# Splitting the scores of a five-block tile into products of 384 and 256 columns

## The chip, the core and the metric

The program runs on one core of a Trainium2 chip. The metric is the time of one execution on the device in microseconds; several executions are timed and their median is given. One further execution was recorded by the hardware profiler, and all rows below come from it.

## What is computed

Two layers over x of shape (2, 1024, 256): a linear attention layer, which the change leaves alone, and a transformer block with causal softmax attention (32 query heads, 8 key/value heads, 64 per head) and a mixture of experts. Each layer is added to x through a layer norm. The part that the change touches:

```python
q = (h @ wq).reshape(b, s, NH, D).transpose(0, 2, 1, 3)
k = (h @ wk).reshape(b, s, NKV, D).transpose(0, 2, 1, 3)
k = jnp.repeat(k, GROUPS, axis=1)            # 4 query heads share a key head
scores = jnp.einsum('bhqd,bhkd->bhqk', q, k) / jnp.sqrt(jnp.float32(D))
scores = jnp.where(causal, scores, jnp.finfo(scores.dtype).min)
attn = jax.nn.softmax(scores, axis=-1)
out = jnp.einsum('bhqk,bhkd->bhqd', attn, v)
```

## The kernel before

Each engine has one program of its own; semaphores order them. The softmax attention is a loop over 16 sequences (8 key/value groups times 2 batches), and each sequence has 8 tiles of 128 queries. Tile t belongs to sequence n = t // 8 and has ct = t % 8 in it; being causal, it attends to ct + 1 blocks of 128 keys. Four heads share each tile. The tile with five blocks is ct = 4.

Step t of the loop on TensorE interleaves three tiles by a fixed order in the source: score(t, 0), values(t - 2), score(t, 1), turn_part(t - 1, 0), score(t, 2), turn_part(t - 1, 1), project_out(t - 2), score(t, 3), turn_part(t - 1, 2), and a projection for a later half sequence. turn_part transposes normalised probabilities, block by block, four heads each (L1346); values multiplies them with v (L1358); project_out is L1367; the projection is L1295, or two transposes at L1285.

A score keeps float32 accuracy by splitting: query and key are each held as a rounded part and its remainder. The stationary operand holds the query's two parts stacked on 128 partitions, and two products accumulate into PSUM, one with khi (L1329) and one with klo (L1330), both of type fp32r. One product can write at most one bank of 512 columns. A tile with up to four blocks has one pair of products of up to 512 columns in a bank of its own per head; a tile with five or more has a pair of 512 columns and a pair with the rest, in two adjoining banks that heads 0 and 2, and 1 and 3, share. khi and klo have place for three halves of a sequence: the first half of even sequences lies at column 0, of odd ones at 512, and the second half of either at 1024 (place_in_half). Blocks 0 to 3 are the first half, block 4 begins the second.

VectorE (DVE) takes each head's scores with one masked maximum (L924), which also moves them to SBUF; ScalarE (ACT) takes the exponential (L673) and copies transposed blocks (L685); DVE normalises (L932). In step t DVE does maximum(t, 0), normalise(t - 1, 2) and (t - 1, 3), a part of the projected item (L907, L912 or L917), maximum(t, 1), maximum(t, 2), normalise(t, 0), the sum of the output (L961), maximum(t, 3), normalise(t, 1). The first transpose of a tile waits until all four heads of it are normalised (semaphore probs_ready). Other products that are named below: L1249 (linear attention) has a moving operand cut in short runs, by `vp[:, b, 4 * k:4 * (k + 1), 0:4:3]`; L1444 is the experts' first product, 128 columns in one run.

Of the kernel before, what the change touches and what calls it, by code (L numbers as in the profile page):

```python
# [14 lines left out]
P = 128  # L15
D = 256
KB = D // P
BATCH, SEQ = 2, 1024
NT = BATCH * SEQ // P
TB = SEQ // P  # L20
# [13 lines left out]
HALF = SEQ // 2  # L34
PAIRS = TB * (TB + 1) // 2
EPS = 1e-5
MASKED = -1e30
# [44 lines left out]
def place_in_half(n, half):  # L82

    return 2 * HALF if half else n % 2 * HALF


def build(nc, a, out):
    ctx = ExitStack()
    with ctx:
# [10 lines left out]
        def turned_bank(t, k):  # L100

            return wide[:, 2 * t + k, :] if t < 2 else bank[2 * (t - 2) + k][:]

        def score_bank(t, h):

            if t % TB < TB // 2:
                return wide[:, h, :]
            return wide[:, 2 * (h % 2):2 * (h % 2) + 2, :].rearrange("p a b -> p (a b)")
# [15 lines left out]
        def S(name):  # L124

            if name not in sems:
                sems[name] = ctx.enter_context(nc.semaphore(name))
            return sems[name]
# [22 lines left out]
        def part(at, n, pattern, **dims):  # L151
            return arena[:, at:at + n].rearrange(pattern, **dims)
# [23 lines left out]
        at = 10 * KB * D  # L176
        n = KB * BATCH * HB * P
# [14 lines left out]
        at = 14336  # L192
# [34 lines left out]
        probs = [part(i * G * SEQ, G * SEQ, "p (h m) -> p h m", h=G) for i in range(2)]  # L227
# [10 lines left out]
        causal = part(4 * G * SEQ + 8 * P, SEQ, "p (o c) -> p (o c)", o=1)  # L238
# [56 lines left out]
        with ExitStack() as early:  # L295
            def sb_early(name, shape, dt):
                return early.enter_context(nc.sbuf_tensor(name, shape, dt))

            khi = sb_early("khi", [P, 3 * HALF], F32R)
            klo = sb_early("klo", [P, 3 * HALF], F32R)  # L300
# [231 lines left out]
        def _(act):  # L532
# [177 lines left out]
            for t in range(NT // 4):  # L710
                act.wait_ge(S("hT_psum"), 2 * t + 1)
                nc.scalar.copy(hT[:, 0, t * 4 * P:(t + 1) * 4 * P], turned_bank(t, 0)).then_inc(S("hT0_ready"), 1)
# [50 lines left out]
        def _(v):  # L763
# [29 lines left out]
            for n in range(4):  # L793
                ins = nc.vector.tensor_tensor(fdiagT[:, n], bank[0][:, n * DK:(n + 1) * DK].rearrange("p (o e) -> p o e", o=1).to_broadcast([P, HB, DK]),
                                              headmask[:].rearrange("p (h o) -> p h o", o=1).to_broadcast([P, HB, DK]), ALU.mult)
# [3 lines left out]
            for k in range(KB):  # L799
                ins = nc.vector.tensor_scalar(gate[:, k], gate[:, k], ln2[:, k:k + 1], None, ALU.mult)  # L800
# [21 lines left out]
            def pair_step(s):  # L822
# [16 lines left out]
                if s == TB + 1:  # L839
                    for h in range(G):  # L840
                        maximum(0, h)
# [79 lines left out]
            def maximum(t, h):  # L921
                w = (t % TB + 1) * P
                v.wait_ge(S("scores2"), G * t + h + 1)
                nc.vector.tensor_tensor_reduce(out=probs[t % 2][:, h, 0:w], in0=score_bank(t, h)[:, 0:w], in1=causal[:, SEQ - w:SEQ], scale=-1.0, scalar=-MASKED,  # L924
                                               op0=ALU.add, op1=ALU.min, accum_out=nmax[:, t % 2, h:h + 1]).then_inc(S("nmax_ready"), 1)

            def normalise(t, h):
# [14 lines left out]
            for t in range(TILES + 2):  # L942
# [14 lines left out]
                if weighing:  # L957
                    n, ct = divmod(t - 2, TB)
                    v.wait_ge(S("proj2"), t - 1)
                    at = acc[:, n % BATCH * TB + ct]  # L960
# [6 lines left out]
            for t in range(NT // 4):  # L967
                v.wait_ge(S("hT_psum"), 2 * t + 2)
                nc.vector.tensor_copy(hT[:, 1, t * 4 * P:(t + 1) * 4 * P], turned_bank(t, 1)).then_inc(S("hT1_ready"), 1)
# [23 lines left out]
            for t in range(NT):  # L993
                ins = nc.vector.max(top[:, t], glog[:, t])
            step(ins)
            for t in range(NT):
                ins = nc.vector.max_index(topi[:, t], top[:, t], glog[:, t])
# [5 lines left out]
            for k in range(TOPK):  # L1003
                ins = nc.vector.tensor_tensor(pick[:, k], experts[:].rearrange("p (e o) -> p e o", o=1).to_broadcast([P, E, NT]),
                                              topf[:, :, k].rearrange("p (o t) -> p o t", o=1).to_broadcast([P, E, NT]), ALU.is_equal)
# [25 lines left out]
                                                in1=place[:], op0=ALU.mult, op1=ALU.add))  # L1031
            step(nc.vector.tensor_tensor(place[:], within, place[:], ALU.add))
            for k in range(TOPK):
                ins = nc.vector.tensor_tensor(prod[:, k], pick[:, k], place[:], ALU.mult)
            step(ins)
            for k in range(TOPK):
                ins = nc.vector.tensor_reduce(row[:, k], prod[:, k].rearrange("p e t -> p t e"), AX.X, ALU.add)
# [9 lines left out]
            def over_slots(x):  # L1047
                return x.rearrange("p (c o) -> p c o", o=1).to_broadcast([P, C, NS])
# [3 lines left out]
            for kk in range(TOPK):  # L1052
                ins = nc.vector.tensor_tensor(worth[:, kk * NT:(kk + 1) * NT, 0], inslot[:, kk * NT:(kk + 1) * NT],
                                              tileno[:].rearrange("p (t o) -> p t o", o=1).to_broadcast([P, NT, NS]), ALU.mult)
# [18 lines left out]
            for i in range(3):  # L1073
                ins = nc.vector.tensor_tensor(worth[:, :, 2 + i], inslot[:], over_slots(wsplit[:, i].rearrange("p k t -> p (k t)")), ALU.mult)
# [16 lines left out]
            for q in range(NT // 2 + 1):  # L1091
                if q < NT // 2:
                    tiles = (2 * q, 2 * q + 1)
                    v.wait_ge(S(f"h_loaded{q // 2}"), 16)
                    for i in tiles:
                        ins = nc.vector.bn_stats(stf[:, i], acc[:, i])
                    ins.then_inc(S("ve_f_st"), 1)
                    v.wait_ge(S("ve_f_st"), q + 1)
                    for i in tiles:
                        ins = nc.vector.bn_aggr(hmean[:, i], stf[:, i])  # L1100
                    ins.then_inc(S("mean_f"), 1)
                if q:
                    cols = slice(2 * q - 2, 2 * q)
# [8 lines left out]
        def _(pe):  # L1112
            mm = nc.tensor.matmul
# [3 lines left out]
            for w, to in ((2, bank[1]), (3, bank[2])):  # L1117
                for k in range(KB):
                    for f in range(KB):
                        ins = nc.tensor.transpose(to[:, (k * KB + f) * P:(k * KB + f + 1) * P], wnat[:, w, f, k * P:(k + 1) * P], ident[:])  # L1120
# [18 lines left out]
            for n in range(4):  # L1139
                if n == 2:  # L1140
                    turn_xn(0)
                for k in range(KB):
                    for f in range(KB):
                        ins = mm(wide[:, n, (k * KB + f) * P:(k * KB + f + 1) * P], wnat[:, n // 2, f, k * P:(k + 1) * P],
                                 fdiagT[:, n].rearrange("p h e -> p (h e)"), start=True, stop=True)
# [152 lines left out]
            def scores_read(t, h):  # L1298

                ct = t % TB  # L1300
                if ct == 0:
                    return G * (t - 1) + 3 + h // 2
                if ct < TB // 2:
                    return G * (t - 1) + h + 1
                if ct == TB // 2 and h < 2:
                    return G * (t - 1) + 2 * h + 2
                return G * t + h - 1

            def score(t, h):
                n, ct = divmod(t, TB)  # L1310
                if ct == 0 and h == 0:
                    pe.wait_ge(S("k_doubled"), n * 2 + 1)
                    pe.wait_ge(S("qlo_ready"), n * 4 + 1)
                if ct == 0 and h == 2:
                    pe.wait_ge(S("qlo_ready"), n * 4 + 2)
                if t == 0 and h == 3:
                    pe.wait_ge(S("v2_ready"), 1)
                if ct == TB // 2 and h == 0:
                    pe.wait_ge(S("k_doubled"), n * 2 + 2)
                    pe.wait_ge(S("qlo_ready"), n * 4 + 4)  # L1320
                if t:
                    pe.wait_ge(S("nmax_ready"), scores_read(t, h))
                w = (ct + 1) * P
                at = place_in_half(n, ct >= TB // 2) + ct % (TB // 2) * P
                q = qhl[:, h, at:at + P]
                for half in range(1 if w <= HALF else 2):
                    lo, cols = place_in_half(n, half), min(w - half * HALF, HALF)
                    dst = score_bank(t, h)[:, half * HALF:half * HALF + cols]
                    mm(dst, q, khi[:, lo:lo + cols], start=True, stop=False)  # L1329
                    ins = mm(dst, q, klo[:, lo:lo + cols], start=False, stop=True)  # L1330
                ins.then_inc(S("scores2"), 1)

            for s in range(TB + 3):
# [61 lines left out]
            for t in range(NT // 4):  # L1395
                for k in range(KB):
                    for q in range(4):
                        ins = nc.tensor.transpose(turned_bank(t, k)[:, q * P:(q + 1) * P], acc[:, 4 * t + q, k * P:(k + 1) * P], ident[:])
                    ins.then_inc(S("hT_psum"), 1)
            pe.wait_ge(S("gate_ready"), 1)  # L1400
            for i in range(NT):
                pe.wait_ge(S("hT0_ready"), i // 4 + 1)
                pe.wait_ge(S("hT1_ready"), i // 4 + 1)
                for k in range(KB):
                    ins = mm(wide[:, 0, i * E:(i + 1) * E], hT[:, k, i * P:(i + 1) * P], gate[:, k], start=(k == 0), stop=(k == KB - 1))
# [8 lines left out]
            for c in range(C):  # L1414
                pe.wait_ge(S("inplace_ready"), c * 4 // C + 1)
                ins = mm(bank[2][:, 0:2 * NS], inplace[:, c], worth[:, c, 0:2].rearrange("p v s -> p (v s)"), start=(c == 0), stop=(c == C - 1))
            ins.then_inc(S("found_psum"), 1)
            pe.wait_ge(S("worth_ready"), 2)
            for c in range(C):
                ins = mm(bank[1][:, 0:3 * NS], inplace[:, c], worth[:, c, 2:5].rearrange("p v s -> p (v s)"), start=(c == 0), stop=(c == C - 1))  # L1420
# [11 lines left out]
            with pe.Fori(0, NS // UR) as it:  # L1432
                for u in range(UR):
# [3 lines left out]
                    for half in range(2):  # L1437
                        for at, w, name in ((0, "w1", "up_psum"), (2, "w3", "gate_psum")):
                            if half == 0:
                                pe.wait_ge(S(f"{w}_loaded{u}"), 16 * it + 16)  # L1440
                            w = w1_e[u] if w == "w1" else w3_e[u]
                            for f in range(4):
                                for k in range(KB):
                                    ins = mm(wide[:, at + half, f * P:(f + 1) * P], w[:, k, (half * 4 + f) * P:(half * 4 + f + 1) * P], sT[u][:, k],  # L1444
                                             start=(k == 0), stop=(k == KB - 1))
# [4 lines left out]
                    for f in range(FB):  # L1450
                        if f % 4 == 0:
                            pe.wait_ge(S("gated_ready"), slot * 2 + f // 4 + 1)
                        ins = mm(bank[u][:, 0:D], gated[:, f], w2_e[u][:, f], start=(f == 0), stop=(f == FB - 1))  # L1453
# [23 lines left out]
```

## Time and profile before

| | us |
|---|---|
| median of 3 timed runs (1827.85 to 1828.76) | 1828.71 |
| the profiled execution | 1825.54 |
| its span, first to last instruction | 1823.6 |
| busy: PE / PEld / DVE / ACT | 1730.6 / 1381.9 / 1035.5 / 1066.2 |

PE is TensorE's products, PEld its weight loads, which run beside them. The shown length of a product holds the way through the array and overlaps the next product's, so prices on TensorE are taken from start to start. In the timeline, instructions of one line in a row are merged: "x4" with one start and the time to the end of the last. An idle time before a piece stands in brackets with what ended it. Idle time of an engine off the chain costs nothing.

### The profile page before, as it was taken

The page shows a single profiled execution, that of the slowest core. Times are in us where ns is not written, and L with a number is a line of the kernel's source. Part 1 is how long each engine was busy: PE and PEld are TensorE (multiplying, and loading weights), DVE is VectorE, ACT ScalarE, POOL GpSimd, SP SyncE. Part 2 cuts the span into 40 slices and gives each one's busy share as a digit, 9 for nine tenths or more (in the row PEclk, how much of TensorE's full clock was granted, in tenths as well). Part 3 has the DMA queues.
Part 4 walks back from the last instruction along what each step waited for, and adds up shares of the span by engine and source line. Part 5 has one row for each costly group of instructions (what it writes and reads, how often), then busy time and mean ns, then how long its engine had stood idle before and what let it go on. Part 6 is the DMA issues. An engine that isn't in the chain of part 4 may idle for free.

```text
span 1823.6 us, 31555 instructions
## 1 busy us (share of the span) xinstructions
PE 1730.6 (95%) x12094; PEld 1381.9 (76%) x12094; DVE 1035.5 (57%) x2595; ACT 1066.2 (58%) x2408; POOL 207.9 (11%) x236
## 2 busy tenths in 40 slices
PE   7999799999999999999999999999949999999993
PEld 6777477777777777777777777777739999999993
DVE  3777667777676677686686677676661111111112
ACT  3344677787777787787787787777731222222223
POOL 2223100000000000000000000000011222222222
PEclk9999899999999999999999999999969999999997
DMA  3000100000000000000000000000053153113533
GB/s 87 1 2 2 47 1 10 1 1 10 1 1 10 1 1 10 1 1 9 2 1 9 1 1 1 1 1 24 1 191 116 23 161 94 26 23 92 156 99 98
DMA packets 46102, 60.17 MB, mean 33 GB/s; under 512 B 8993, under 2 KB 39585, under 8 KB 45985
## 3 DMA queue, kind: packets, MB, share of 16 engines
q1 hardware_dynamic: 35088, 46.15, 7.5%
q0 software_dynamic: 7536, 10.36, 3.4%
q10 hardware_dynamic: 3360, 2.10, 0.4%
q8 instruction: 73, 1.20, 0.3%
q14 instruction: 45, 0.36, 0.1%
HBM read 138.43 MB, written 11.40 MB: 82 GB/s over the span
## 4 chain that ended last, share of the span: by engine, by line
PE 86%; DVE 10%; ACT 2%; POOL 1%; issue 1%; DMA 1%; ACTq 0%; POOLq 0%; DVEq 0%
PE wide L1444 15%; PE bank L1346 13%; PE bank L1358 12%; PE bank L1295 9%; PE bank L1453 7%; PE wide L1329 7%; PE wide L1330 6%; PE bank L1367 5%; PE bank L1156 3%; DVE arena L924 2%; DVE arena L932 2%; DVE qhl L917 1%; ACT arena L673 1%; PE wide L1168 1%; PE bank L1242 1%
## 5 line engine op out<-in xcount | busy, mean ns | idle before, releaser
L924 DVE CUSTOM_DVE_ANT_0 arena<-wide,arena 128x896 f32<-128x896 f32 (+7 forms) x512 | 382.9, 755 | 241.1 <-PE wide L1330 234.7
L673 ACT ACTIVATE arena<-arena,nmax 128x896 f32<-128x896 f32 (+7 forms) x512 | 399.0, 780 | 87.8 <-DVE nmax L924 85.1
L685 ACT COPY arena<-bank 128x512 f32<-128x512 f32 x576 | 311.7, 586 | 82.6 <-PE bank L1346 77.1
L1329 PE MATMUL wide<-khi,qhl 128*128 128x512 f32 (+3 forms) x768 | 344.5, 450 | 1.3 <-DVE vt L907 1.3
L1346 PE MATMUL bank<-ident,arena 128*128 128x128 f32 x2304 | 309.3, 274 | 7.5 <-DVE arena L932 6.4
L1444 PEld LDWEIGHTS wide<-wo,arena 128*128 128x128 f32 x2496 | 284.8, 192 | 3.3 <-issue 1.3
L1346 PEld LDWEIGHTS bank<-ident,arena 128*128 128x128 f32 x2304 | 259.8, 140 | 34.6 <-issue 21.2
L1444 PE MATMUL wide<-wo,arena 128*128 128x128 f32 x2496 | 285.1, 275 | 0.9 <-ACT wo L729 0.9
L1358 PE MATMUL bank<-arena,vt 128*64 128x256 f32 x2304 | 276.9, 385 | 0.0
L932 DVE TENSOR_SCALAR arena<-arena,rinv 128x896 f32<-128x896 f32 (+7 forms) x512 | 258.0, 525 | 9.1
L1088 DVE TENSOR_TENSOR wo<-wide,wo 128x512 f32<-128x512 f32 x78 | 53.9, 692 | 365.9 <-PE wide L1444 365.9
L1330 PE MATMUL wide<-klo,qhl 128*128 128x512 f32 (+3 forms) x768 | 256.7, 347 | 0.0
L1358 PEld LDWEIGHTS bank<-arena,vt 128*64 128x64 f32 x2304 | 154.2, 136 | 90.7 <-issue 19.5
L1329 PEld LDWEIGHTS wide<-khi,qhl 128*128 128x128 f32 x768 | 145.5, 189 | 87.2 <-issue 64.8
L1330 PEld LDWEIGHTS wide<-klo,qhl 128*128 128x128 f32 x768 | 146.1, 190 | 37.3 <-issue 22.5
L739 ACT ACTIVATE wo<-wide 128x512 f32<-128x512 f32 x78 | 46.6, 597 | 168.2 <-PE wide L1444 168.2
L1453 PE MATMUL bank<-arena,wo 128*128 128x256 f32 x624 | 141.1, 379 | 0.0
L1367 PE MATMUL bank<-wo,oT 128*128 128x256 f32 x512 | 134.2, 385 | 0.9 <-ACT oT L695 0.9
L479 POOL CAST khi<-khi 64x512 fp32r<-64x512 f32 x32 | 19.5, 608 | 973.7 <-ACT khi L661 973.6
L1453 PEld LDWEIGHTS bank<-arena,wo 128*128 128x128 f32 x624 | 115.5, 190 | 14.1
L1295 PE MATMUL bank<-rT_all,wq_g 128*128 128x512 f32 x248 | 116.7, 593 | 0.0
L673 ACT ACTIVATION_READ_ACCUMULATOR arena<-arena,nmax 128x1 f32 x512 | 98.8, 193 | 0.0
(232 smaller groups left out, 1572.3 us busy)
## 6 DMA issues: line engine op xcount, KB each, us to landing
arena<-in_L_ffn_w SPq DMA_DIRECT2D x117, 1024.0 KB
wq_g<-in_L_ffn_wq SPq DMA_DIRECT2D x8, 256.0 KB, 3.0
wo<-in_L_ffn_wo SPq DMA_DIRECT2D x16, 128.0 KB, 2.9
hbuf<-acc SPq DMA_DIRECT2D x2, 1024.0 KB, 4.5
tbuf<-rT_all SPq DMA_DIRECT2D x4, 512.0 KB, 3.0
acc<-hbuf SPq DMA_DIRECT2D x4, 512.0 KB, 5.4
out<-x_all SPq DMA_DIRECT2D x8, 256.0 KB, 2.1
x_all<-in_L_attn_x ACTq DMA_DIRECT2D x2, 896.0 KB, 8.5
```

Source lines behind the costliest of these rows:

```text
L673: nc.scalar.activation(probs[t % 2][:, h, 0:w], probs[t % 2][:, h, 0:w], ACT.Exp, bias=nmax[:, t % 2, h:h + 1], scale=-1.0, accum_out=rsum ...
L685: nc.scalar.copy(pT[t % 2][m], bank_of((t, m))).then_inc(S("pT_ready"), 1)
L924: nc.vector.tensor_tensor_reduce(out=probs[t % 2][:, h, 0:w], in0=score_bank(t, h)[:, 0:w], in1=causal[:, SEQ - w:SEQ], scale=-1.0, scalar ...
L932: nc.vector.tensor_scalar(probs[t % 2][:, h, 0:w], probs[t % 2][:, h, 0:w], rinv[:, t % 2, h:h + 1], None, ALU.mult).then_inc(S("probs_rea ...
L1295: ins = mm(to, w, rT_all[:, k, at:at + HALF], start=(k == 0), stop=(k == KB - 1))
L1329: mm(dst, q, khi[:, lo:lo + cols], start=True, stop=False)
L1330: ins = mm(dst, q, klo[:, lo:lo + cols], start=False, stop=True)
L1346: ins = nc.tensor.transpose(to[:, h * P:(h + 1) * P], probs[t % 2][:, h, m * P:(m + 1) * P], ident[:])
L1358: ins = mm(bank[2][u * DH:(u + 1) * DH, 0:2 * P], vt[:, n % 2, m], pT[t % 2][m][:, u * 2 * P:(u + 1) * 2 * P], start=(m == 0), stop=(m == ct))
L1367: ins = mm(bank[2][:, 2 * P:2 * P + D], oT[:, j], wo2[:, t // (BATCH * TB), j], start=(j == 0), stop=(j == 1))
L1444: ins = mm(wide[:, at + half, f * P:(f + 1) * P], w[:, k, (half * 4 + f) * P:(half * 4 + f + 1) * P], sT[u][:, k], start=(k == 0), stop=(k ...
L1453: ins = mm(bank[u][:, 0:D], gated[:, f], w2_e[u][:, f], start=(f == 0), stop=(f == FB - 1))
```

## The change

For tiles with five blocks the scores of a head are laid at columns 128 to 767 of their pair of banks in place of 0 to 639, so that the first bank takes three blocks (384 columns) and the second two (256). DVE's maximum reads from there. Blocks 3 and 4 of the keys belong to different halves: in odd sequences they adjoin (896 and 1024), in even ones they lie five blocks apart (384 and 1024), and the product takes them with a step. Operands of every score product are now written as blocks of 128 columns; sizes and places of all other tiles are as they were.

```diff
--- before.py
+++ after.py
@@ -100,6 +100,11 @@
         def turned_bank(t, k):
 
             return wide[:, 2 * t + k, :] if t < 2 else bank[2 * (t - 2) + k][:]
+
+        def scores_of(t, h):
+
+            at = P if t % TB == TB // 2 else 0
+            return score_bank(t, h)[:, at:at + (t % TB + 1) * P]
 
         def score_bank(t, h):
 
@@ -921,7 +926,7 @@
             def maximum(t, h):
                 w = (t % TB + 1) * P
                 v.wait_ge(S("scores2"), G * t + h + 1)
-                nc.vector.tensor_tensor_reduce(out=probs[t % 2][:, h, 0:w], in0=score_bank(t, h)[:, 0:w], in1=causal[:, SEQ - w:SEQ], scale=-1.0, scalar=-MASKED,
+                nc.vector.tensor_tensor_reduce(out=probs[t % 2][:, h, 0:w], in0=scores_of(t, h), in1=causal[:, SEQ - w:SEQ], scale=-1.0, scalar=-MASKED,
                                                op0=ALU.add, op1=ALU.min, accum_out=nmax[:, t % 2, h:h + 1]).then_inc(S("nmax_ready"), 1)
 
             def normalise(t, h):
@@ -1323,11 +1328,19 @@
                 w = (ct + 1) * P
                 at = place_in_half(n, ct >= TB // 2) + ct % (TB // 2) * P
                 q = qhl[:, h, at:at + P]
-                for half in range(1 if w <= HALF else 2):
-                    lo, cols = place_in_half(n, half), min(w - half * HALF, HALF)
-                    dst = score_bank(t, h)[:, half * HALF:half * HALF + cols]
-                    mm(dst, q, khi[:, lo:lo + cols], start=True, stop=False)
-                    ins = mm(dst, q, klo[:, lo:lo + cols], start=False, stop=True)
+                if ct < TB // 2:
+                    parts = [(0, w)]
+                elif ct == TB // 2:
+                    parts = [(0, 3 * P), (3 * P, w)]
+                else:
+                    parts = [(0, HALF), (HALF, w)]
+                for first, end in parts:
+                    blocks = [place_in_half(n, x >= TB // 2) // P + x % (TB // 2) for x in range(first // P, end // P)]
+                    step = blocks[-1] - blocks[0] if ct == TB // 2 and first else 1
+                    keys = slice(blocks[0], blocks[-1] + 1, step)
+                    dst = scores_of(t, h)[:, first:end].rearrange("p (b c) -> p b c", c=P)
+                    mm(dst, q, khi[:].rearrange("p (b c) -> p b c", c=P)[:, keys], start=True, stop=False)
+                    ins = mm(dst, q, klo[:].rearrange("p (b c) -> p b c", c=P)[:, keys], start=False, stop=True)
                 ins.then_inc(S("scores2"), 1)
 
             for s in range(TB + 3):
```

## Rows read from the trace of the kernel before

**Rows 1.** Page, the chain that ended last, share of the span by engine

```profile
PE 86%; DVE 10%; ACT 2%; POOL 1%; issue 1%; DMA 1%; ACTq 0%; POOLq 0%; DVEq 0%
```

**Rows 2.** Stages: us, busy us (instructions) of PE, PEld, DVE, ACT, POOL, PEclk, DMA

```profile
218.00:1299.00 1081.00, 1074.01 (x6837) 791.55 (x6836) 788.90 (x2034) 836.15 (x1876) 36.56 (x60) 1.00 0.02 4
...
711.91:720.71 8.80, 8.43 (x55) 6.40 (x54) 7.58 (x21) 7.49 (x18) 0.00 (x0) 1.00 0.00 0
641.57:650.37 8.80, 8.43 (x55) 6.41 (x54) 7.57 (x21) 7.49 (x18) 0.00 (x0) 1.00 0.01 2
```

**Rows 3.** Waits of PE, 218 to 1299 us: total us, times, longest

```profile
PE bank L1346 <- DVE arena L932: 5.9, 16, 0.4
```

**Rows 4.** Timeline of PE, 711.91 to 720.71 us: start, us, engine, line, operation

```profile
715.44 0.63 PE L1346 MATMUL bank<-ident,arena 128*128 128x128 f32 x4 [0.37 <-DVE arena L932]
715.83 0.48 PE L1329 MATMUL wide<-khi,qhl 128*128 128x512 f32 x1
...
716.37 0.22 PE L1329 MATMUL wide<-khi,qhl 128*128 128x128 f32 x1
716.43 0.28 PE L1330 MATMUL wide<-klo,qhl 128*128 128x128 f32 x1
...
717.00 1.03 PE L1367 MATMUL bank<-wo,oT 128*128 128x256 f32 x4
717.68 0.58 PE L1329 MATMUL wide<-khi,qhl 128*128 128x512 f32 x1
...
719.40 1.88 PE L1295 MATMUL bank<-rT_all,wkv_g 128*128 128x512 f32 x4
```

**Rows 5.** Chain that ended last, pieces from 706 to 717 us

```profile
706.66 0.25 PE wide L1330
...
714.41 0.89 DVE arena L932 x2
```

**Rows 6.** Timeline of PE, the next tile, six blocks

```profile
724.62 0.60 PE L1346 MATMUL bank<-ident,arena 128*128 128x128 f32 x4
724.97 0.48 PE L1329 MATMUL wide<-khi,qhl 128*128 128x512 f32 x1
...
725.76 1.04 PE L1346 MATMUL bank<-ident,arena 128*128 128x128 f32 x8
726.63 1.03 PE L1367 MATMUL bank<-wo,oT 128*128 128x256 f32 x4
727.31 0.59 PE L1329 MATMUL wide<-khi,qhl 128*128 128x512 f32 x1
...
729.08 1.88 PE L1295 MATMUL bank<-rT_all,wq_g 128*128 128x512 f32 x4
```

**Rows 7.** Timeline of PE, head 3 of tiles with three and four blocks

```profile
703.58 0.52 PE L1329 MATMUL wide<-khi,qhl 128*128 128x384 f32 x1
...
704.55 1.88 PE L1295 MATMUL bank<-rT_all,wq_g 128*128 128x512 f32 x4
...
710.69 0.58 PE L1329 MATMUL wide<-khi,qhl 128*128 128x512 f32 x1
...
711.77 0.38 PE L1285 MATMUL bank<-ident,vT 128*128 128x128 f32 x2
```

**Rows 8.** Timeline of DVE, 712 to 725 us

```profile
712.47 0.68 DVE L924 CUSTOM_DVE_ANT_0 arena<-wide,arena 128x512 f32<-128x512 f32 x1
...
713.47 0.82 DVE L924 CUSTOM_DVE_ANT_0 arena<-wide,arena 128x640 f32<-128x640 f32 x1
...
722.02 0.96 DVE L924 CUSTOM_DVE_ANT_0 arena<-wide,arena 128x768 f32<-128x768 f32 x1 [2.02 <-PE wide L1330]
...
723.10 1.02 DVE L932 TENSOR_SCALAR arena<-arena,rinv 128x640 f32<-128x640 f32 x2
```

**Rows 9.** Timeline of PE, products of L1249 and of L1444

```profile
169.09 1.05 PE L1249 MATMUL bank<-arena,wo 128*128 128x128 f32 x8
...
1399.73 2.29 PE L1444 MATMUL wide<-wo,arena 128*128 128x128 f32 x19
```

## The prediction

> **What bounds the kernel now.** I read the page's shares of the chain that ended last first: 86% PE and 10% DVE [rows 1]. So a saving on TensorE counts wherever the chain is on TensorE, and is lost in the 10% where it is on VectorE. The table by stage says where the change lies: the attention loop, 218 to 1299 us, at a granted clock of 1.00 (the 2.4 GHz level), PE busy for 1074.0 of 1081.0 us [rows 2]. TensorE's list of waits for that stage has a single entry: the transposes of L1346 wait for DVE L932, 5.9 us in 16 waits of at most 0.4 [rows 3]. There are 16 sequences (8 groups x 2 batches), each with one tile of five blocks, so that is one wait in each such tile's step; the timeline of TensorE shows where it stands [rows 4].
>
> One step is one tile: the scores of tile t, the transposes of t-1, the values of t-2. I use the step that starts at 711.91 (sequence 7); the same window for a step of an even sequence has the same length, 8.80 us, and the same busy times to 0.02 us [rows 2]. In it TensorE runs head 0, twelve value products, head 1, then stands until 715.44 (gap 0.37) for DVE L932, then four transposes, head 2, four more transposes, L1367, head 3, eight transposes, the projection [rows 4]. The chain through it leaves TensorE after head 0 of the tile before (706.66 + 0.25) and stays on DVE, once on ACT, over 28 pieces of which the last is 714.41 + 0.89, until it comes back to TensorE at 715.44 [rows 4, 5]. Heads 0 and 1 of the five-block tile are not on it. Heads 2 and 3, and all that follows until the next tile of four blocks, are.
>
> **The change part by part.** (1) Per head, the two products of 512 columns become two of 384, and the two of 128 become two of 256; count of products, columns, weight loads and semaphore steps stay the same. Their price is taken from start to start, as the shown durations overlap. Head 2 of the five-block tile runs from 715.83 to 717.00, 1.17 us with its four transposes [rows 4]. Head 2 of the six-block tile (512 and 256 columns) runs from 724.97 to 726.63, 1.66 us with eight transposes; these take 0.87 us, 0.109 each, so with four it would be 1.225 [rows 6]. Hence 128 more columns in both *second* products cost 0.055 in all. The price of 128 columns in both *first* products comes from head 3 of the tiles of four and three blocks: 710.69 to 711.77 is 1.08, 703.58 to 704.55 is 0.97, so 0.11 us [rows 7]. The new head is 1.225 - 0.11 = 1.115, that is 0.055 less than 1.17. Head 3 in the same way: 717.68 to 719.40 is 1.72 now [rows 4]; with 512 and 256 it is 1.77, from 727.31 to 729.08 [rows 6]; 1.77 - 0.11 = 1.66, 0.06 less.
>
> Why the same columns cost less: the 128-column product that begins at 716.37 is followed after 0.06 us, but the next, at 716.43, is followed only after 0.11 (four transposes from there to 717.00 at 0.109 and a start 0.02 late make up the rest of 0.57) [rows 4], which is the spacing of the transposes too, though these have only 128 columns at a rate at which 128 columns could pass in 0.055. Each product comes with a weight load of its own, and a product shorter than the load behind it leaves the array waiting. At 256 columns, 0.11 by the price of rows 7, stream and load are about equal, so nothing is left waiting.
>
> The Trainium skill, "TensorE: Matmul & The Clock Gate", section "LDWEIGHTS (loading the stationary operand)", puts a load at columns divided by 1.2, an estimate of 107 ns for 128; the trace agrees with 109. The same page's section "Back-to-back issue gap" speaks against the change: its gap for one product grows linearly with columns, so 512 + 128 and 384 + 256 come out equal and the sum would be zero instead of the saving above. The 0.055 against 0.11 of the rows contradicts it here; it is a rival below all the same.
>
> (2) Heads 0 and 1: the same arithmetic gives 0.055 each on TensorE, but they end before the wait, whose end DVE sets. DVE's queue holds the maximum of head 0 (713.47, with no idle time before it) and then the two normalisations of the old tile that release the transposes; none of it waits for heads 0 or 1 [rows 5, 8]. I cost this saving at nothing: the wait grows from 0.37 to about 0.48. If that cover were gone they would bring 16 x 0.11 = 1.8 us more.
>
> (3) The scores lie 128 columns further right, so L924's maximum reads columns 128 to 767 of its pair of banks. Width and number of reads are unchanged; 640 columns cost 0.82 and 512 cost 0.68 [rows 8]. A shifted start is not in the trace. Its bounds: nothing below, and above, the step of one width of 128, 0.14 us, for the one such maximum on the DVE chain (head 0): 16 x 0.14 = 2.2 us. I take zero, as neither the size nor the pair of banks changes.
>
> (4) In even sequences blocks 3 and 4 of the keys are not adjacent, so the 256-column products read two runs of 128 columns. The nearest row is L1249, whose moving operand is cut into eight runs of 16 columns: eight in 1.05 us with a last one of 0.275, spacing 0.111, against 0.112 for the plain L1444 (19 in 2.29) [rows 9]. So zero. Upper end: such a product falls to the rate of L1367, that the 4-byte operands of L1444 have, 0.112 for 128 columns, 0.22 for 256 in place of 0.12 [rows 9]; then 0.1 x 2 products x 2 heads x 8 sequences = 3.2 us.
>
> (5) What is late next behind the saving: in the next step the transposes at 724.62 need the last normalisation of the five-block tile, which ends at 723.10 + 1.02 = 724.12 [rows 6, 8]. It follows the maximum at 722.02, before which DVE idled until TensorE's head 0, so it moves with TensorE; even standing still it leaves 0.50 less the 0.14 from the end of a normalisation to the transposes it releases (715.30 to 715.44, rows 4 and 5), 0.36 us for a shift of 0.115.
>
> Sum: 16 x (0.055 + 0.06) = 1.8 us. The profiled execution took 1825.54 (span 1823.6 and 1.9 around it); it would take 1823.7. The median of the timed runs is 1828.71, 3.2 above it, and I carry the difference over: 1826.9.
>
> **The rivals.**
> A, the cover is not one: heads 0 and 1 count too, 3.6 us in all, 1825.1. For it: only that shares of a wait inferred from one execution can hide a second condition. Against: the unbroken DVE run of rows 5.
> B, the split is neutral: a product costs its columns and nothing else, 0.11 for two times 128 anywhere; then the head stays at 1.17 and the time at 1828.7. For it: from 716.37 to 716.43 the first 128-column product costs just its columns [rows 4]. Against: the second pair's 0.055 [rows 4, 6]. The Trainium skill's gap formula, named above, gives this case.
> C, the two runs of keys stream at the slow rate in even sequences: +3.2 - 1.8, 1830.1. Against it stands L1249.
> D, slower: the keys are now cut into blocks of 128 for every tile's products. If the pattern stays in pieces also where the blocks are adjacent, every product pays at each turn from one block to the next. Place: all 1536 score products with 36 x 16 x 4 x 2 = 4608 blocks, so 3072 turns. At x ns per turn the result is 3.07x - 1.8 us: it cancels the saving at 0.6 ns, and is slower by 0.2% from 1.8 ns. At 2 ns it would be +4.3, 1833.0. Against: L1249's seven turns cost under 2 ns together [rows 9].
> E, the change does not do what it says (the shapes stay, or loads still trail): no change, inside B.
>
> **How the numbers follow.** A measurement of this kernel can tell about 0.2%, 3.7 us, from no change. Forecast 0.70 (1826.9); A 0.12 (1825.1, so half its chance is faster by over 0.2%); B with E 0.09; C 0.04; D 0.05. Faster by over 0.2%: 0.06 from A and 0.02 from the edge of the forecast, 0.08. Slower: D and 0.01 of C, 0.06. Within 0.2%: 0.86. The range takes in A, B and the bound of (3), 1829.1, with 0.7 us on each side for the spread of the medians (the runs lie 0.9 apart): 1824.4 to 1829.8; it leaves out D, C and little else.
>
> **What would show it.** In the profile after: forms of 128x384 and 128x256 each x64 more under the two score lines, 512 and 128 each x64 fewer; head 2 of a five-block tile 1.11 to 1.12 us where it was 1.17; its step 8.80 - 0.115 = 8.69 us; the 16 waits on DVE L932 grown from 5.9 to 7.0 to 7.7 us; steps of all other tiles unchanged. Longer spacing of 384-column products than 0.18 would show D, steps of even and odd sequences that differ would show C, an unchanged wait with a step shortened by 0.22 would show A. The prediction would be wrong if the wait in the step vanished, or if the L924 maximum of 640 columns took longer than 0.82.

## The result and the profile after

The median of 22 timed runs is 1825.69 us (1823.4 to 1826.71) against 1827.91 (1825.57 to 1829.16) for 22 runs of the kernel before on the same chips. The ratio is 0.9986, 95% interval [0.998, 0.9992]: about 2.6 us or 0.14% by the ratio, 2.2 us by the two medians. The forecast was 1.8 us or 0.10%, from 1828.71 to 1826.9. So the kernel is a little faster, and by less than the 0.2% that the prediction named as what a measurement can tell; the 44 runs tell it.

In the profiled execution the span is 1823.3 us, where it was 1823.6; nearly all of the gain is missing there. The stages show why, and they come first.

Two steps of a five-block tile, and the step that follows the first of them; columns as in rows 2:

```profile
781.43:790.09 8.66, 8.19 (x55) 6.39 (x54) 7.55 (x21) 7.50 (x18) 0.00 (x0) 1.00 0.01 2
641.06:649.72 8.66, 8.19 (x56) 6.38 (x54) 7.55 (x21) 7.50 (x18) 0.00 (x0) 1.00 0.01 2
790.09:799.73 9.64, 9.64 (x62) 7.29 (x61) 7.24 (x16) 8.09 (x18) 1.22 (x2) 1.00 0.00 1
```

8.66 stands against 8.80 [rows 2]. The next step, a six-block tile, had 9.68 in the kernel before:

```profile
791.05:800.73 9.68, 9.68 (x62) 7.29 (x61) 7.24 (x16) 8.08 (x18) 1.22 (x2) 1.00 0.00 1
```

The same timeline of TensorE as in rows 4, after the change, for the step at 781.43:

```profile
784.21 0.28 PE L1343 MATMUL wide<-klo,qhl 128*128 128x256 f32 x1
784.96 0.63 PE L1359 MATMUL bank<-ident,arena 128*128 128x128 f32 x4 [0.47 <-DVE arena L937]
785.34 0.42 PE L1342 MATMUL wide<-khi,qhl 128*128 128x384 f32 x1
785.60 0.34 PE L1343 MATMUL wide<-klo,qhl 128*128 128x384 f32 x1
785.77 0.28 PE L1342 MATMUL wide<-khi,qhl 128*128 128x256 f32 x1
785.89 0.28 PE L1343 MATMUL wide<-klo,qhl 128*128 128x256 f32 x1
786.00 0.60 PE L1359 MATMUL bank<-ident,arena 128*128 128x128 f32 x4
786.44 1.03 PE L1380 MATMUL bank<-wo,oT 128*128 128x256 f32 x4
787.12 0.52 PE L1342 MATMUL wide<-khi,qhl 128*128 128x384 f32 x1
...
788.77 1.88 PE L1300 MATMUL bank<-rT_all,wkv_g 128*128 128x512 f32 x4
```

The transposes still begin 3.53 us after the step's first product (784.96 less 781.43; before, 715.44 less the step's start at 711.91, rows 2 and 4), so heads 0 and 1 brought nothing; the gap has grown from 0.37 to 0.47. Head 2 takes 785.34 to 786.44, 1.10 us in place of 1.17, head 3 1.65 in place of 1.72 [rows 4]; in the median of the 15 steps that have a projection (the last sequence's has none) head 2 goes from 1.18 to 1.10 and head 3 from 1.72 to 1.66. Under the two score lines the forms of 384 and of 256 columns went from 128 to 192 products each, those of 512 from 384 to 320 and those of 128 from 128 to 64, as forecast, so rival E is out. All waits of TensorE in the loop, us in total, times, longest:

```profile
PE bank L1359 <- DVE arena L937: 7.6, 16, 0.5
```

They were 5.9 [rows 3]. From head 0 of the second tile to head 0 of the last, the loop took 1096.78 us before (202.44 to 1299.22) and 1094.12 after (203.09 to 1297.21): 2.66 less. In this execution 0.65 of it went to a later start of the loop and 1.7 was given back behind it. Two stretches of TensorE, the experts' first products, after the change and then before it:

```profile
1370.89 9.07 PE L1457 MATMUL wide<-wo,arena 128*128 128x128 f32 x64 [0.90 <-ACT wo L734]
```

```profile
1372.97 7.41 PE L1444 MATMUL wide<-wo,arena 128*128 128x128 f32 x64 [0.90 <-ACT wo L729]
```

The work begins 2.1 us earlier but needs 1.7 us more for the first 64 products. The table by stage has the reason in its clock column, for 1372.60 to 1374.40, again after and then before:

```profile
1372.60:1374.40 1.80, 1.80 (x10) 1.80 (x10) 0.00 (x0) 0.00 (x0) 0.00 (x0) 0.50 1.02 394
```

```profile
1372.60:1374.40 1.80, 1.43 (x12) 1.43 (x13) 0.00 (x0) 0.13 (x1) 0.94 (x1) 1.00 1.01 405
```

In the profile after, the granted clock was still at 0.50 (1.2 GHz) when the experts' loop had begun; before, it had risen to 1.00 (2.4 GHz) by then. It had fallen at 1330.03 (before: 1331.62), while TensorE ran the 64 small products of the gate (8 columns each), and stayed low through routing, where TensorE was mostly idle. The change does not decide when it comes back: among the fourteen profiles of this document both the early and the late return are found with kernels that have the change and with kernels that lack it (last section). The medians of many runs carry the gain, a single span does not.

### The profile page after: what moved, and what is told of

Read it like the earlier page. It is cut to its first block, busy times and chain, and to the rows that moved or that the text cites. A ratio compares the mean times of both kernels' runs of the same rounds, so it can differ in the third digit from the quotient of the medians.

```text
span 1823.3 us, 31555 instructions
## 1 busy us (share of the span) xinstructions
PE 1727.5 (95%) x12094; PEld 1382.5 (76%) x12094; DVE 1035.4 (57%) x2595; ACT 1067.1 (59%) x2408; POOL 207.9 (11%) x236
## 4 chain that ended last, share of the span: by engine, by line
PE 85%; DVE 10%; ACT 2%; POOL 1%; issue 1%; DMA 1%; ACTq 0%; POOLq 0%; DVEq 0%
PE wide L1457 15%; PE bank L1359 13%; PE bank L1371 12%; PE bank L1300 9%; PE bank L1466 7%; PE wide L1342 7%; PE wide L1343 6%; PE bank L1380 5%; PE bank L1161 3%; DVE arena L929 2%; DVE arena L937 2%; DVE qhl L922 1%; ACT arena L678 1%; PE wide L1173 1%; PE bank L1247 1%
```

## The experiments

The steps below are read from head 0 of one tile to head 0 of the next; the last sequence's step of a five-block tile has no projection and is left out. In each run the other 15 lie within 0.04 us of each other, and the medians of the four runs with the same heads 2 and 3 (after, full, heads23, six384) are all 8.66 or 8.67, so a profile decides questions that the time of a run can't. "Loop" is the distance defined above.

**The change again, beside its two halves.** The diff of the halves, here for heads 0 and 1 (the other has `h >= 2`); the last line keeps the step between blocks off the heads that are left at 512 + 128:

```diff
-            at = P if t % TB == TB // 2 else 0
+            at = P if t % TB == TB // 2 and h < 2 else 0
...
-                elif ct == TB // 2:
+                elif ct == TB // 2 and h < 2:
...
-                    step = blocks[-1] - blocks[0] if ct == TB // 2 and first else 1
+                    step = blocks[-1] - blocks[0] if ct == TB // 2 and first == 3 * P else 1
```

> The changed kernel again, on one chip with the next three. Both theories: ratio 0.9986 to the kernel before, 2 to 3 us. Its profile: step of a five-block tile 8.66 to 8.69 us against 8.80, waits on the normalisation grown from 5.9 to 7.6 us. The clock's return before the experts' loop may again differ between executions, so the span may hide this gain.

> Only heads 0 and 1 of the five-block tile are split 384 + 256; heads 2 and 3 keep 512 + 128. Cover theory: they finish before DVE's normalisation lets the transposes go, so the step stays 8.80 us, the 16 waits grow from 5.9 to about 7.6 us, and the time does not change (within 0.3 us, ratio 1.000). Rival A (heads 0 and 1 count too): step 8.69, 1.8 us less, ratio 0.999.

> Only heads 2 and 3 are split 384 + 256. Cover theory: all of the gain is here: step 8.66 to 8.69 us as in the full change, waits unchanged at 5.9 us, time 1.8 to 2.6 us less, ratio 0.9986 to 0.999. Rival A: half of the gain, step 8.73, 1.0 to 1.3 us less.

The full change: 1824.68 us, ratio 0.9981 [0.9972, 0.999] to the kernel before (1827.88). Heads 0 and 1 alone: 1828.04, 1.0003 [0.9994, 1.0012]. Heads 2 and 3 alone: 1825.47, 0.9984 [0.9975, 0.9993]. The steps, heads 0 and 1 alone, then heads 2 and 3 alone:

```profile
712.22:721.03 8.81, 8.33 (x55) 6.36 (x54) 7.58 (x21) 7.50 (x18) 0.00 (x0) 1.00 0.00 0
```

```profile
712.08:720.75 8.67, 8.30 (x56) 6.45 (x54) 7.57 (x21) 7.50 (x18) 0.00 (x0) 1.00 0.00 0
```

And their waits, in the same order:

```profile
PE bank L1359 <- DVE arena L937: 7.6, 16, 0.5
```

```profile
PE bank L1359 <- DVE arena L937: 5.9, 16, 0.4
```

Splitting heads 0 and 1 lengthens the wait by exactly what the full change does and leaves the step where it was; the loop is 1096.65 against 1096.78. Splitting heads 2 and 3 leaves the wait and gives the whole gain, loop 1094.15 against 1094.12 for all four. Rival A falls: the gain is all in heads 2 and 3.

**The cover taken away.** The wait ends with a chain on DVE. To shorten or remove it without touching TensorE, the normalisation of four-block tiles was cut to 128 of its 512 columns, with the kernel before and with the changed one as base. The other three blocks stay unnormalised, so a part of the softmax is left out. First for heads 2 and 3:

```diff
-                nc.vector.tensor_scalar(probs[t % 2][:, h, 0:w], probs[t % 2][:, h, 0:w], rinv[:, t % 2, h:h + 1], None, ALU.mult).then_inc(S("probs_ready"), 1)
+                wn = P if t % TB == TB // 2 - 1 and h >= 2 else w
+                nc.vector.tensor_scalar(probs[t % 2][:, h, 0:wn], probs[t % 2][:, h, 0:wn], rinv[:, t % 2, h:h + 1], None, ALU.mult).then_inc(S("probs_ready"), 1)
```

> The kernel before, but the normalisation of heads 2 and 3 of four-block tiles does only 128 of 512 columns (the other three blocks of these heads stay unnormalised, so a part of the softmax is left out). This takes some 0.6 us of DVE work from the chain ahead of the wait in the five-block step. Cover theory: the wait disappears, step 8.80 to about 8.27 us, 8 us less. It is the base for the next run.

> The changed kernel with the same shortened normalisation (the same part of the softmax left out). Without the wait all four heads count. Cover theory: against the run before it the step is shorter by 0.22 to 0.24 us and the time by 3.5 to 3.8 us, nearly twice what the change brings with the wait. Rival (heads 0 and 1 are worth nothing for another reason, such as the order of value products behind them): the same 0.14 us and 2.2 us as with the wait.

Measured 1820.99 us (ratio 0.9962 [0.9949, 0.9976]) and 1817.13 (0.9947 [0.9933, 0.996]), both to the kernel before, 1827.79. But the five-block step was 8.40, not 8.27, and 8.27 in the second; the loop went from 1089.95 to 1087.72, 2.2 us, which is what the rival of this pair gives. The medians are 3.9 apart, which would have fitted the cover, but part of that can be the clock of TensorE: in the first profile it came back 3.9 us after the experts' first product, in the second 0.7 us before it. The list of waits was empty in both, though the transposes began 0.24 and 0.36 us after head 1's last product where 0.11 and 0.12 is the closest spacing (the first of the two below): the list counts idle time from the shown end of a product, 0.28 us after its start, so it misses a wait that this length covers or nearly covers. The wait was not gone; a normalisation of 128 columns still starts 0.20 us behind the one before it, 512 columns 0.40. This pair could not decide, and the gap of its steps, 0.13 us, is only that of heads 2 and 3.

```profile
711.89 0.27 PE L1331 MATMUL wide<-klo,qhl 128*128 128x128 f32 x1
712.13 0.63 PE L1347 MATMUL bank<-ident,arena 128*128 128x128 f32 x4
```

So all four heads were cut (without `and h >= 2`):

> The kernel before with the normalisation of all four heads of a four-block tile cut to 128 of 512 columns (the other three blocks stay unnormalised, a part of the softmax is left out). The first relief took 0.40 us off the DVE chain where 0.53 were needed, so a wait of 0.13 us was left. Four short ones take about 0.8 us off. Cover theory: transposes follow head 1 at once (0.11 us after its last product), step 8.80 to 8.27 us, loop 8.5 us shorter.

> The changed kernel with the same cut (the same part of the softmax left out). Cover theory: no wait is left in either of the two, so all four heads count: the step is shorter than in the run before it by 0.21 to 0.24 us (8.04 to 8.06 us), the loop by 3.5 to 3.8 us. If heads 0 and 1 are worth nothing for another reason: by 0.13 us and 2.2 us, as in the first pair of reliefs.

Measured 1817.43 us (0.9943 [0.9929, 0.9956]) and 1813.89 (0.9923 [0.991, 0.9937]), the kernel before at 1827.92. The two steps, of the kernel before and of the changed one under this cut:

```profile
708.43:716.70 8.27, 8.27 (x55) 6.34 (x53) 6.96 (x21) 7.40 (x18) 0.00 (x0) 1.00 0.00 0
```

```profile
706.02:714.05 8.03, 8.03 (x55) 6.40 (x54) 6.97 (x21) 7.41 (x18) 0.00 (x0) 1.00 0.01 2
```

Head 1 and the transposes behind it, in the same order:

```profile
711.32 0.27 PE L1331 MATMUL wide<-klo,qhl 128*128 128x128 f32 x1
711.43 0.63 PE L1347 MATMUL bank<-ident,arena 128*128 128x128 f32 x4
```

```profile
708.80 0.28 PE L1344 MATMUL wide<-klo,qhl 128*128 128x256 f32 x1
708.92 0.60 PE L1360 MATMUL bank<-ident,arena 128*128 128x128 f32 x4
```

0.11 and 0.12 us: nothing is waited for any more. The median step goes from 8.26 to 8.00, the loop from 1088.15 to 1083.84, 4.3 us. With the wait the same change is worth 2.7. The difference, 1.6 us or 0.10 per step, is what heads 0 and 1 are worth when uncovered (predicted 0.11 and 1.8); by the five-block steps alone it is 0.26 less 0.14, 0.12 per step, as the six-block steps, below, do not gain the same in the two pairs.

**The price of a size.** The second pair of products widened, the first left at 512:

```diff
-                    lo, cols = place_in_half(n, half), min(w - half * HALF, HALF)
+                    lo, cols = place_in_half(n, half), min(w - half * HALF + (P if ct == TB // 2 else 0), HALF)
```

> The kernel before with one size changed: the second pair of products of a five-block tile has 256 columns in place of 128 (the sixth block of keys is computed too and nobody reads it), the first pair stays 512. Load theory (a product of 128 columns takes as long as the weight load behind it, about 0.11): heads 2 and 3 grow by 0.047 to 0.055 us each, step 8.80 to 8.90, 1.5 to 1.8 us more in all, though 2 x 128 columns per head at 0.055 each are 0.11. Rival B (a product costs its columns): heads grow by 0.11 each, step 9.02, 3.5 us more.

Measured 1828.64 us, 1.0003 [0.9994, 1.0012] to 1827.88. The step and head 2:

```profile
714.04:722.93 8.89, 8.64 (x55) 6.50 (x54) 7.52 (x21) 7.50 (x18) 0.00 (x0) 1.00 0.01 2
```

```profile
717.96 0.47 PE L1329 MATMUL wide<-khi,qhl 128*128 128x512 f32 x1
...
719.18 1.03 PE L1367 MATMUL bank<-wo,oT 128*128 128x256 f32 x4
```

256 columns more in head 2 cost 1.22 less 1.17, 0.05 us, and the step grows by 0.09. Columns alone would be 0.11 and 0.22. Rival B falls. The loop grows by 1.1 us, to 1097.84, where 1.5 to 1.8 were expected: the five-block steps bring 1.4, and the six-block steps behind them give 0.3 back.

**Order of the short products.** Same sizes as before the change; only the four products of a five-block head change places (hi and lo are khi and klo). The kernel before has them as 512 hi, 512 lo, 128 hi, 128 lo. They are written as a list of (which of the pairs, lo or hi), and this is it for the interleaved kernel; the other has (1, 0), (1, 1), (0, 0), (0, 1).

```diff
+                products = [(half, k) for half in halves for k in (0, 1)]
+                if ct == TB // 2:
+                    products = [(0, 0), (1, 0), (0, 1), (1, 1)]
```

> The kernel before with the four products of a five-block head in the order 512 hi, 128 hi, 512 lo, 128 lo in place of 512, 512, 128, 128. Load theory: each short product is followed by an instruction whose load takes 0.11, so the loss of 0.05 is paid twice, once per short product: head 2 grows by 0.02 to 0.08 us over 1.17, step 8.84 to 8.96. If short products lose only when two follow each other: head 2 falls to about 1.12, step 8.70. If nothing but columns counts: no change.

> The kernel before with the 128-column pair ahead of the 512-column pair. Load theory: the short pair now stands behind the transposes, all spaced by their loads, three spacings of 0.11 with two of short products in them, and the long pair follows at 0.23 each: head 2 of the five-block tile 1.19 to 1.22 us in place of 1.17, step 8.84 to 8.90. Columns only: 1.17 and 8.80.

Interleaved: step 8.76 and loop 1095.77, 1.0 us *less* than before (0.6 of it in the five-block steps, 0.4 in the six-block steps behind them), in a single run of 1827.48 us. Short first: step 8.86, loop 1097.42, 0.6 more, in a single run of 1829.15 us. The second is inside what the load theory gave, the first outside everything expected. Head 2 interleaved, where the two products of one source line, 512 and 128 columns, are merged under the first one's form:

```profile
645.87 0.54 PE L1333 MATMUL wide<-khi,qhl 128*128 128x512 f32 x2
646.24 0.51 PE L1333 MATMUL wide<-klo,qhl 128*128 128x512 f32 x2
646.58 0.60 PE L1349 MATMUL bank<-ident,arena 128*128 128x128 f32 x4
647.02 1.03 PE L1370 MATMUL bank<-wo,oT 128*128 128x256 f32 x4
```

The pair that starts at 646.24 is over after 0.34 us. A pair of 512 and 128 columns would stream in 0.23 + 0.06 = 0.29, so the long product behind a short one started or ran 0.05 late. That is the loss at the first short product, as expected. At the second, which the transposes follow, almost nothing is lost: 646.58 to 647.02 is 0.44, four spacings of 0.11. In the old order the same four took 0.46 and followed after 0.11 instead of 0.06 [rows 4]. So my statement that each short product costs 0.05 was wrong. Against the 1.10 us of the changed head 2, two in a row cost 0.08 ahead of transposes (the old order) and 0.10 ahead of a long product (short first, 1.20), one between long ones 0.05, one ahead of transposes about 0.01.

The weight loads show why two in a row lose. These are the loads of head 2 with the short pair first, for 128, 128, 512 and 512 columns:

```profile
717.15 0.19 PEld L1333 LDWEIGHTS wide<-khi,qhl 128*128 128x128 f32 x1
717.26 0.19 PEld L1333 LDWEIGHTS wide<-klo,qhl 128*128 128x128 f32 x1
717.37 0.19 PEld L1333 LDWEIGHTS wide<-khi,qhl 128*128 128x128 f32 x1
717.48 0.19 PEld L1333 LDWEIGHTS wide<-klo,qhl 128*128 128x128 f32 x1
```

They start 0.11 apart, though the 128 columns of each of the first two products could stream in 0.06, and nowhere in the loops of before, after and these two kernels does the load of a score follow that of another in less than 0.108. The loads of a transpose are shorter, 0.14 us shown against 0.19, and the closest two of them start 0.06 apart. That fits their hiding behind a short product; no run took it apart.

**Two parts that are both long enough.** For odd sequences, the six-block tile split 384 + 384 in place of 512 + 256:

```diff
-            at = P if t % TB == TB // 2 else 0
+            at = P if t % TB == TB // 2 or (t % TB == TB // 2 + 1 and t // TB % 2) else 0
-                elif ct == TB // 2:
+                elif ct == TB // 2 or (ct == TB // 2 + 1 and n % 2):
```

> The changed kernel, with tiles of six blocks in odd sequences split 384 + 384 in place of 512 + 256 as well. Load theory: no product of either split is shorter than its load, so the split is neutral: steps of six-block tiles 9.64 us in odd and even sequences. If evenness of the two parts as such were worth something: a shorter step in odd sequences, by up to 0.2 us.

One run of 1825.49 us; the step with the new split:

```profile
720.31:729.95 9.64, 9.64 (x62) 7.40 (x61) 7.24 (x16) 8.08 (x18) 1.22 (x2) 1.00 0.01 3
```

9.64 as with 512 + 256 in the changed kernel. In this run the even sequences, which keep 512 + 256, lie between 9.64 and 9.67, the odd ones between 9.64 and 9.65, so evenness is worth nothing that this spread of 0.03 us would not hide; getting above 128 columns is what counts.

**A version that beats both.** Since the DVE chain decides when the transposes may start, one of its pieces went to GpSimd, which is idle there. To the changed kernel it adds a piece on GpSimd, once per sequence, leaves head 1 of four-block tiles out of DVE's normalise, and has TensorE wait for both (one more wait, of GpSimd for its own piece ahead of its work for the next sequence, is not printed):

```diff
+                t = n * TB + TB // 2 - 1
+                gp.wait_ge(S("k_doubled"), 2 * n + 2)
+                gp.wait_ge(S("rinv_ready"), 2 * t + 1)
+                nc.gpsimd.tensor_scalar(probs[t % 2][:, 1, 0:HALF], probs[t % 2][:, 1, 0:HALF], rinv[:, t % 2, 1:2], None, ALU.mult).then_inc(S("pool_probs"), 1)
...
+                if t % TB == TB // 2 - 1 and h == 1:
+                    return
...
-                        pe.wait_ge(S("probs_ready"), G * (t + 1))
+                        pe.wait_ge(S("probs_ready"), G * (t + 1) - (t + TB // 2 + 1) // TB)
+                        if t % TB == TB // 2 - 1:
+                            pe.wait_ge(S("pool_probs"), t // TB + 1)
```

> The changed kernel, with the normalisation of head 1 of each four-block tile on GpSimd (idle there) in place of DVE; nothing is left out. DVE's chain ahead of the wait loses one normalisation of 0.40 us, but then the exponential of head 3 on ACT ends last. Cover theory: transposes start 0.18 to 0.3 us earlier in 16 steps, 3 to 4.5 us less than the changed kernel, ratio to the kernel before about 0.9965. Rival: GpSimd takes over 2 us for 512 columns, or slows DVE at the memory they share, and the step gets longer than 8.66.

Measured 1820.53 us, ratio 0.9958 [0.9944, 0.9972] to the kernel before (1827.92). The step, GpSimd's piece in it, and the end of the DVE chain:

```profile
710.20:718.65 8.45, 8.19 (x56) 6.39 (x54) 7.25 (x20) 7.43 (x18) 1.74 (x1) 1.00 0.00 0
```

```profile
710.16 1.78 POOL L511 TENSOR_SCALAR arena<-arena,rinv 128x512 f32<-128x512 f32 x1 [16.26 <-DVE rinv L950]
```

```profile
712.33 0.17 DVE L950 RECIPROCAL rinv<-rsum 128x2 f32<-128x2 f32 x1
712.53 0.88 DVE L945 TENSOR_SCALAR arena<-arena,rinv 128x512 f32<-128x512 f32 x2
```

GpSimd takes 1.78 us for what DVE starts anew every 0.40, but is done 1.6 us before the transposes need it. The step falls by 0.21 and the loop from 1094.12 to 1090.59. Of the 0.40 us taken from DVE, 0.21 arrives; the rest went to the next in line, as expected: DVE now stands idle ahead of the reciprocal at 712.33 until ACT has the exponential of head 3. TensorE's remaining gap is shown as 0.26 us in each of the 16 steps.

## Why the prediction was right

**What bounds the kernel** held. The stretch that DVE carries ends 3.53 us into the five-block step, with the change as without. The two halves of the change show it directly, and the pair without the wait gives the uncovered price.

**Part (1)**, the price per head: 0.055 for head 2 and 0.06 for head 3 were forecast, 0.08 and 0.06 came in the median (0.07 and 0.07 in the step shown). The neighbours in rows 6 and 7 were the right ones. The short term is the second pair: its cost of 128 more columns was read as 0.055, and wide768, which changes it alone, has 0.04 to 0.05 per head; with the 0.11 of the first pair that makes 0.07. The step went from 8.80 to 8.66, forecast 8.69.

Of the reason that was given, one step is not shown. The prediction read the transposes' spacing of 0.109 as that of their weight loads, "at a rate at which 128 columns could pass in 0.055". That is the rate of the scores. The transposes are of type f32, and by its own part (4) other f32 products take about 0.11 for 128 columns, so their columns alone could explain 0.109, and their loads can follow each other in 0.06. What the runs show is a pace of 0.11 for the loads of scores, and that a short product ahead of a transpose need not pay for it (interleaved).

**Part (2)**, nothing from heads 0 and 1: confirmed, and the wait grew from 5.9 to 7.6 us, inside 7.0 to 7.7. **Parts (3) and (4)**, zero: confirmed, as the step came out 0.03 us below the forecast and not above it. The maximum of 640 columns starting at column 128 still takes 0.82 us, and even and odd sequences have like steps (both kinds lie between 8.66 and 8.69), so rival C is out; the second product of 384 columns takes 0.17 to 0.18 from start to start, so D is out too.

```profile
782.99 0.82 DVE L929 CUSTOM_DVE_ANT_0 arena<-wide,arena 128x640 f32<-128x640 f32 x1
```

**Part (5)** said that nothing else moves, and the forecast said that steps of all other tiles stay unchanged. That was wrong by 0.03 us in the six-block step. Summed over the loop, the five-block steps gained 2.14 us (forecast 1.84), the six-block steps 0.47 and all others 0.05: 2.66, so the larger part of the 0.8 us that the sum missed lies outside the changed tile. The products of that step are the same; head 0 is shorter by 0.007 us, head 1 by 0.009 and head 3 by 0.018. What decides it stays open. It is not simply the absence of 128-column products in heads 2 and 3 of the tile before: full, heads23 and wide768 have it in the median without them, but relief_after, without them too, has 9.67 in eleven of 15 steps; and with them the interleaved kernel has 9.65, and relief2_before 9.64 in six of its 15 steps and 9.68 in nine.

**Carrying the difference to the median** worked for the median: 1826.9 was forecast and 1825.69 came, and of the 1.2 us between them 0.8 is only that 22 runs of the kernel before have their median at 1827.91, where three had 1828.71. For the single execution it failed: the profiled one took 1825.20 us, 1823.7 was forecast. Of the 2.66 us gained in the loop, 0.65 went to a later start of the loop and 1.7 to what is behind it, which is what the first 64 products of the experts needed more at the lower clock. The profiled execution before, at 1825.54 us, was one with the early return of the clock and as fast as the fastest of the 22 runs (1825.57); the one after had the late return.

## What to carry to other kernels

When a product must be cut at a bank's limit, cut it so that no part streams in less time than the weight loads need between them, here 0.06 us for 128 columns against 0.11: 512 + 128 lost 0.07 us per head against 384 + 256, and 512 + 256 against 384 + 384 nothing that could be measured. Read from the chain which instances of a repeated saving lie ahead of a wait that another engine ends: half of this one was worth nothing there. That other chain, once named, was worth more than the change: one instruction moved to an idle engine brought 3.5 us in the loop, though it took about four times as long there.

## What the runs showed of the hardware that was not expected

A short product's loss depends on what follows it: 0.05 us ahead of a long score product, about 0.01 ahead of transposes when it stands alone between long ones. The order of equal products alone moved the loop by -1.0 or +0.6 us, in one profile each.

Nearly the whole wait of TensorE can be missing from the list of waits: 0.13 us of it were not shown at all in relief_before, as the shown end of a product lies 0.28 us after its start, and 0.53 us were shown as 0.37 in the kernel before.

The granted clock came back from 0.50 to 1.00 at either of two places. In three of the fourteen profiles (before, relief_after, relief2_after) that was 0.4 to 1.1 us ahead of the experts' first product, in the other eleven 3.5 to 4.7 us behind it; in the kernels before and after at 1372.58 and 1374.40 us. Early: the first 64 products took 7.41 us. Late: 9.07 with 3.5 us of them at 0.50 (1370.89 to 1374.40), so 1.7 more, not far from what the change brings; and 9.65 in the second profile of the changed kernel (full), where 4.7 us were at 0.50:

```profile
1371.30 9.65 PE L1457 MATMUL wide<-wo,arena 128*128 128x128 f32 x64 [0.90 <-ACT wo L734]
```

```profile
1370.00:1376.00 6.00, 5.10 (x24) 4.71 (x23) 0.68 (x3) 1.22 (x3) 0.94 (x1) 0.50 1.03 392
```

What decides between early and late is not shown.
